# Second modulation moved behind the transposes, twelve row places, and new orders on all engines of an AdaLN block with experts

## The chip, the cores and the metric

The kernel runs on one core of one Trainium2 chip. TensorE (PE) multiplies, VectorE (DVE) and ScalarE (ACT) work elementwise, GpSimd (POOL) does small elementwise work and issues the indirect DMAs, SyncE (SP) issues most other DMAs. The metric is the device time of one execution in microseconds (us), the median of several; lower is better.

## What is computed

The input x is 2 batches x 2048 tokens x 128 channels. Cut to what matters:

```
mod = (silu(c) @ wmod).reshape(2, 6, 1, 128);  sa, ca, ga, sb, cb, gb = mod's six parts
ga, gb = sign * maximum(abs(.), 0.25)
h = layernorm(x) * (1 + ca) + sa
gate_x, gate_a = sigmoid(h @ w_in), sigmoid(h @ w_a)        # block diagonal, 8 blocks
log_a = -8 * softplus(a_param) * gate_a;  a = exp(log_a)
b = sqrt(1 - exp(2 * log_a)) * (gate_x * h)
x = x + ga * scan(a, b)                                     # y[t] = a[t] * y[t-1] + b[t]
h = layernorm(x) * (1 + cb) + sb
logits = silu(h @ rw1 + rb1) @ rw2 + rb2                    # 128 -> 512 -> 8 experts
top two experts per token, weights = softmax of the two logits
out = sum over both of weight * (silu(h @ w1[e] + b1[e]) @ w2[e] + b2[e])   # 128 -> 512 -> 128
x = x + gb * out
```

"Second modulation" is the step `* (1 + cb) + sb` on the second h. cb and sb differ by batch.

## The kernel before

**Tiles.** The 4096 tokens are 8 groups (g) of 512, four tiles of 128 tokens each; groups 0 to 3 are batch 0, groups 4 to 7 batch 1. Everything up to the experts (the head) goes by groups: LN1 statistics (`stats1`), 1/sigma (`rstd1`, POOL), normalising (`norm1`: groups 0 to 2 on POOL, the rest on DVE), transposes (`turn_x`, PE), first modulation out of PSUM (`modulate`, ACT), two gate products (`gates`, PE), `tanh` and `decay` (ACT), 1 - exp (`clamp`, an ACT Relu) and its root (`mult`, ACT), gated input and `scan` (DVE), transposes back (`turn_y`), residual and LN2 statistics (`resid`, DVE). LN2's normalising is `norm2` (DVE): two passes over each 128-token tile, L816 with 1 + cb spread over all tokens (`cbB`) and L823 with 1/sigma and sb (`sbB`). The result lies by tokens in `rows`, already modulated. It is turned (`turn_h`), copied out of PSUM by ACT (`copy`, L626), and goes through the router (`router`, `silu`, `logits`, `lgc`, `sum`). `top2` (DVE) picks two experts, `rank` (PE) counts, and `place` (DVE) works out for every token and choice a row in `sorted_rows` in HBM. POOL sends the rows there: `send`, 64 indirect DMAs at L550, each of 128 rows; those of a group wait for its `place`.

**Experts.** The sorted rows make 39 tiles of 256 rows, each for one expert. Tiles 0 to 8 hold rows of groups 0 to 3 alone (all batch 0), and can run before the second half is routed. For tile s: SP loads the rows into one of U = 10 places of `xr` (L411; a place is free when the scatter of the tile that used it has landed), PE turns them (`tx`, L1194) into bank 1, DVE copies them to `xT` (L986), and copies the expert's weights (`w1` L995, `w2` L1004; both need a register load from the table `tab`, L979), PE does layer 1 (`l1`, L1205), ACT Silu (`hid`, L657), PE layer 2 (`l2`, L1218), ACT the bias (`yb`, L666), PE turns back (`ty`, L1226) into the same bank 1, DVE scales (`sc`, L1012), POOL scatters to `expert_out` by two indirect DMAs (L559). `tx` waits until bank 1 was read by the `sc` ahead of it, `ty` until it was read by the `xT` ahead of it.

**Order.** Each engine's order is written out by hand in a table PLAN (names as above, the number is the group or tile). It ends with tile 10; then each engine runs fixed steps: 20 steps in a hardware loop, the others written out. A step s is, on PE, `tx` s+1, `l1` s, `ty` s-2, `l2` s-1; on DVE `xT` s+1, `w1` s+1, `sc` s-2, `w2` s; on ACT `yb` s-2, `hid` s. In six late steps DVE also sums up finished groups (`combine`, L1031 to L1033). A waiting instruction blocks all that stands behind it on its engine.

The reader will need these lines:

```
FIRST = 11            # first step outside PLAN
pe.wait_ge(TILE_READ[...], ...)      # ty waits s_xT, tx waits s_yo: both use bank 1
if not (static(s) and s < U):
    sp.wait_ge(s_sc[u], 16 * HALVES * (rounds(s, u) - 1))     # a load waits for its place
```

## Time and profile before

| | |
|---|---|
| median of 3 runs | 290.06 us (289.06 to 291.38) |
| profiled execution | 288.09 us, span in the trace 286.2 us |
| PE busy | 248.1 us (87%), 1179 matmul records |
| DVE busy | 188.4 us (66%), 750 instructions |
| ACT busy | 166.5 us (58%), 322 instructions |
| POOL busy | 171.6 us (60%), 192 instructions |

The profile also gives the busy share of each engine in 40 equal slices of the span (9 is 90% or more) and the granted TensorE clock in tenths:

```profile
PE   7767759997599798999999999999999999989910
DVE  3959999999999987576444444444444446866533
ACT  4189979999785355545555555555555556445300
POOL 4996211267777757777777777644554445645650
PEclk9997979999779799999999999999999999999995
```

One slice is 7.2 us. The head takes the first 15 slices or so, and the expert tiles most of the rest.

### The profile page before, as it was taken

To read this page: it belongs to the slowest core of one execution; us is meant where nothing else is said; L and a number is where in the kernel's file an instruction comes from. 1 tells how busy PE (TensorE), PEld (TensorE's weight loads), DVE (VectorE), ACT (ScalarE), POOL (GpSimd) and SP (SyncE) were. 2 spreads that over 40 slices of the span, in tenths; PEclk is the share of its full clock that TensorE was granted. 3 is DMA by queue.
4 is the path that set the end of the run, shared out by engine and by line. 5 is a ranking of instruction groups with operands and counts; after the bars stand their busy time and mean duration, and the time that the engine had idled before them with its cause. 6 is when DMAs were issued, how large, how long until landed. Compare 5 with 4: busy or idle time off the path is not lost.

```text
span 286.2 us, 4950 instructions
## 1 busy us (share of the span) xinstructions
PE 248.1 (87%) x1179; PEld 178.0 (62%) x1179; DVE 188.4 (66%) x750; ACT 166.5 (58%) x322; POOL 171.6 (60%) x192
## 2 busy tenths in 40 slices
PE   7767759997599798999999999999999999989910
PEld 6424334444144245687878888888888888868700
DVE  3959999999999987576444444444444446866533
ACT  4189979999785355545555555555555556445300
POOL 4996211267777757777777777644554445645650
PEclk9997979999779799999999999999999999999995
DMA  7993011121131226413533333222217822280505
GB/s 222 308 333 117 19 40 38 37 75 50 55 121 48 89 82 157 114 47 115 149 84 85 111 101 109 57 75 75 74 46 214 221 72 74 84 256 4 161 0 147
DMA packets 45365, 30.51 MB, mean 107 GB/s; under 512 B 5085, under 2 KB 41999, under 8 KB 45342
## 3 DMA queue, kind: packets, MB, share of 16 engines
q1 hardware_dynamic: 40432, 21.75, 27.9%
q0 software_dynamic: 4544, 8.47, 9.0%
q8 instruction: 8, 0.13, 0.2%
q14 instruction: 15, 0.12, 0.2%
q10 hardware_dynamic: 366, 0.04, 0.1%
HBM read 16.39 MB, written 12.67 MB: 102 GB/s over the span
## 4 chain that ended last, share of the span: by engine, by line
PE 40%; POOL 27%; issue 14%; DVE 12%; DMA 4%; POOLq 1%; DVEq 0%; SPq 0%; ACT 0%
POOL sorted_rows L550 21%; PE bank L1218 18%; PE bank L1205 18%; POOL shared L514 3%; PE bank L1226 3%; PE bank L1194 2%; DVE st L698 2%; DMA expert_out<-shared,tx 2%; POOL rs L506 1%; DVE shared L718 1%; POOL expert_out L559 1%; DVE tx L792 1%; DMA xs<-in_L_attn_x_dram 1%; DVE xs L803 1%; DMA tx<-sorted_rows 1%
## 5 line engine op out<-in xcount | busy, mean ns | idle before, releaser
L559 POOL DMA_INDIRECT expert_out<-shared,tx x78 | 80.4, 1031 | 52.9 <-DVE shared L1012 37.4
L657 ACT ACTIVATE hT<-bank,w_t 128x256 f32<-128x256 f32 x156 | 65.4, 470 | 29.3 <-PE bank L1205 28.3
L550 POOL DMA_INDIRECT sorted_rows<-rows,sloti x64 | 63.9, 999 | 27.2 <-issue 18.3
L1205 PE MATMUL bank<-xT,w_t 128*128 128x256 f32 x312 | 74.1, 380 | 0.1
L1218 PE MATMUL bank<-hT,w_t 128*128 128x256 f32 x312 | 74.1, 380 | 0.0
L1205 PEld LDWEIGHTS bank<-xT,w_t 128*128 128x128 f32 x312 | 56.3, 190 | 6.8 <-DVE w_t L995 0.7
L1218 PEld LDWEIGHTS bank<-hT,w_t 128*128 128x128 f32 x312 | 56.2, 190 | 6.2
L666 ACT ACTIVATE yT<-bank,w_t 128x256 f32<-128x256 f32 x39 | 18.4, 473 | 47.6 <-PE bank L1218 47.6
L1134 PE MATMUL bank<-h2T,rw_s 128*128 128x512 f32 x64 | 36.8, 677 | 1.7 <-ACT qv L644 1.4
L986 DVE COPY xT<-bank 128x256 f32<-128x256 f32 x39 | 16.5, 422 | 23.6 <-PE bank L1194 23.6
L1012 DVE TENSOR_TENSOR shared<-bank,tx 128x256 f32<-128x256 f32 x39 | 16.5, 423 | 21.3 <-PE bank L1226 21.2
L995 DVE COPY w_t<-w_s 128x516 f32 x39 | 17.2, 442 | 16.7 <-issue 15.9
L1004 DVE COPY w_t<-w_s 128x513 f32 x39 | 17.3, 443 | 15.3 <-issue 14.4
L1134 PEld LDWEIGHTS bank<-h2T,rw_s 128*128 128x128 f32 x64 | 10.8, 205 | 14.4 <-issue 5.9
L698 DVE BATCH_NORM_STATS2 st<-xs 128x6 f32<-128x128 f32 x64 | 15.7, 282 | 4.2 <-DMA xs<-in_L_attn_x_dram 4.1
L1226 PE MATMUL bank<-ident,yT 128*128 128x128 f32 x78 | 15.2, 276 | 2.5 <-ACT yT L666 1.1
L1194 PE MATMUL bank<-ident,tx 128*128 128x128 f32 x78 | 15.2, 276 | 1.8 <-DMA tx<-sorted_rows 1.3
L1226 PEld LDWEIGHTS bank<-ident,yT 128*128 128x128 f32 x78 | 10.3, 141 | 8.3 <-issue 3.3
L1194 PEld LDWEIGHTS bank<-ident,tx 128*128 128x128 f32 x78 | 10.4, 141 | 7.7 <-DMA tx<-sorted_rows 2.3
L644 ACT ACTIVATE qv<-bank,smallbT 128x512 f32<-128x512 f32 x16 | 10.8, 686 | 6.3 <-PE bank L1134 6.2
L506 POOL TENSOR_TENSOR rs<-ve,half_neg 128x4 f32<-128x4 f32 x8 | 9.3, 1164 | 8.0 <-DVE ve L705 8.0
L542 POOL TENSOR_TENSOR rs<-ve,half_neg 128x4 f32<-128x4 f32 x4 | 4.1, 1035 | 15.7 <-DVE ve L705 15.7
(194 smaller groups left out, 328.9 us busy)
## 6 DMA issues: line engine op xcount, KB each, us to landing
tx<-sorted_rows SPq DMA_DIRECT2D x39, 130.0 KB, 2.2
w_s<-in_L_ffn_w_dram SPq DMA_DIRECT2D x16, 256.0 KB, 6.1
xs<-in_L_attn_x_dram SPq DMA_DIRECT2D x8, 256.0 KB, 5.2
rows<-rows SPq DMA_DIRECT2D x8, 256.0 KB, 2.6
av<-expert_out SPq DMA_DIRECT2D x8, 256.0 KB, 3.7
qv<-expert_out SPq DMA_DIRECT2D x6, 256.0 KB, 5.0
expert_out<-shared,tx POOLq DMA_INDIRECT x78, 2.3
sorted_rows<-padr SPq DMA_DIRECT2D x9, 130.0 KB, 3.0
```

The lines of the kernel that those rows point to most:

```text
L550: p.indirect_dma_start(sorted_rows[:, :], bass.IndirectOffsetOnAxis(ap=sloti[:, k, t:t + 1], axis=0), rows[:, t, k, :], None).then_inc(s_d ...
L559: p.indirect_dma_start(expert_out[:, :], bass.IndirectOffsetOnAxis(ap=xr_i[:, s % U, n, D + 1:D + 2], axis=0), yo[:, s % U, n, :], None, b ...
L657: ins = nc.scalar.activation(hsT[:, u % 2, h, :], bank[4 + q][:, (h % 2) * SL:(h % 2 + 1) * SL], ACT.Silu, bias=w1_t[:, u % 2, HID + h:HID ...
L666: nc.scalar.activation(yT[:, u % 2, :], bank[7][:, 0:SL], ACT.Identity, bias=w2_t[:, u % 2, HC * D:W2E]).then_inc(s_yT_e, 1)
L698: ins = v.bn_stats(st[:, t, :], xs[:, t, :])
L995: v.tensor_copy(w1_t[:, u % 2, :], w1_s[:, bass.ds(e * WE, WE)]).then_inc(s_w1t, 1)
L1004: v.tensor_copy(w2_t[:, u % 2, :], w2_s[:, bass.ds(e * W2E, W2E)]).then_inc(s_w2t, 1)
L1134: t.matmul(bank[2 + n % 2][:, :], rw1_s[:, h * P:(h + 1) * P], h2T[:, g % 2, :], start=True, stop=True).then_inc(s_rl1, 1)
L1194: ins = t.transpose(bank[1][:, n * P:(n + 1) * P], xr[:, u, n, 0:D], ident[:, :])
L1205: ins = t.matmul(bank[4 + h // 2][:, (h % 2) * SL:(h % 2 + 1) * SL], w1_t[:, u % 2, h * P:(h + 1) * P], xT[:, u % 2, :], start=True, stop= ...
L1218: ins = t.matmul(bank[7][:, 0:SL], w2_t[:, u % 2, h * D:(h + 1) * D], hsT[:, u % 2, h, :], start=(h == 0), stop=(h == HC - 1))
L1226: ins = t.transpose(bank[1][:, n * P:(n + 1) * P], yT[:, u % 2, n * P:(n + 1) * P], ident[:, :])
```

## The change

1. **Second modulation on turned tiles.** `norm2` is now one pass (subtract mean, times 1/sigma), so `rows` holds unmodulated values; `sbB` and `cbB` are gone. In the turned layout cb and sb are one value per partition (`gac[:, 3]`, `modc[:, 3]`, from two small products `mod2`). The router's `copy` becomes an ACTIVATE with scale and bias, and `xT` a TENSOR_SCALAR instead of a COPY.
2. **Split column.** A tile from 9 on may hold rows of both batches. `xT` then takes two instructions: all 256 columns with batch 0's values, and again from column k on with batch 1's, k read into a register from a third row of `tab`. `table1` to `table3` have a few instructions more for it.
3. `w2` copies move from DVE to ACT.
4. **Twelve places** for loaded rows (SLOTS), so tiles 10 and 11 wait for no scatter; from tile 12 on the distance is ten as before. PLAN reaches one tile further.
5. `norm1` on POOL is now that of groups 4, 5 and 6. `clamp` of groups 0 to 3 is a POOL minimum with 1.0 (L534 of the changed kernel), with the rest folded into `mult`.
6. The unread products that open the program (`warm`) are 1 + 1 + 1 with 512 columns instead of 4 + 4 + 3 with 128.
7. PLAN is another order on every engine.

The core of the diff:

```diff
-    FIRST = 11
+    FIRST = 12
+    SLOTS = 12
-                turn_x:0 gates:0 turnb:0 turn_x:1 gates:1 turn_x:2 turn_x:3 gates:2 turn_x:4 turn_y:0
+                turn_x:0 turn_x:1 gates:0 gates:1 turn_x:2 mod2:0 turnb:0 turn_x:3 gates:2 gates:3
...
+            def slot(s):
+                return U + s if s < SLOTS - U else s % U
...
+            def no_more_than_one(g):
+                pool.wait_ge(s_exp, g + 1)
+                p.tensor_scalar(qv[:, cols(g)], qv[:, cols(g)], 1.0, None, ALU.min).then_inc(s_up, 1)
...
             def router_copy(g):
...
-                nc.scalar.copy(h2T[:, g % 2, :], turn_bank("turn_h", g)[:, :]).then_inc(s_h2T, 1)
+                nc.scalar.activation(h2T[:, g % 2, :], turn_bank("turn_h", g)[:, :], ACT.Identity,
+                                     bias=modc[:, 3, b:b + 1], scale=gac[:, 3, b:b + 1]).then_inc(s_h2T, 1)
...
+            def weights2(s, u):                                  # on ScalarE
+                e = act.value_load(tab[0:1, 1, bass.ds(s, 1)], min_val=0, max_val=NE - 1)
+                nc.scalar.copy(w2_t[:, u % 2, :], w2_s[:, bass.ds(e * W2E, W2E)]).then_inc(s_w2t, 1)
...
             def ln2_norm(g):
-                    ins = v.scalar_tensor_tensor(rows[:, t, 0, 0:D], xs[:, t, :], mv2[:, t, 0:1], cbB[:, b, :],
-                                                 ALU.subtract, ALU.mult)
-                yield from link(ins)
-                    ins = v.scalar_tensor_tensor(rows[:, t, 0, 0:D], rows[:, t, 0, 0:D], rs2[:, t:t + 1],
-                                                 sbB[:, b, :], ALU.mult, ALU.add)
+                    ins = v.tensor_scalar(rows[:, t, 0, 0:D], xs[:, t, :], mv2[:, t, 0:1], rs2[:, t:t + 1],
+                                          ALU.subtract, ALU.mult)
...
             def take_x(s, u):
-                v.tensor_copy(xT[:, u % 2, :], bank[1][:, 0:SL]).then_inc(s_xT, 1)
+                early = static(s) and s < EARLY
+                v.tensor_scalar(xT[:, u % 2, 0:SL], bank[1][:, 0:SL], gac[:, 3, 0:1], modc[:, 3, 0:1],
+                                ALU.mult, ALU.add).then_inc(s_xT if early else s_xa, 1)
+                if not early:
+                    k = dve.value_load(tab[0:1, 2, bass.ds(s, 1)], min_val=0, max_val=SL)
+                    dve.wait_ge(s_xa, s - EARLY + 1)
+                    v.tensor_scalar(xT[:, u % 2, bass.ds(k, SL)], bank[1][:, bass.ds(k, SL)], gac[:, 3, 1:2],
+                                    modc[:, 3, 1:2], ALU.mult, ALU.add).then_inc(s_xT, 1)
...
             def keep_warm(n):
-                for _ in range((4, 4, 3)[n]):
-                    t.matmul(bank[4][:, 0:P], ident[:, :], ident[:, :], start=True, stop=True)
+                for _ in range((1, 1, 1)[n]):
+                    t.matmul(bank[4][:, :].rearrange("p (k q) -> p k q", q=P), ident[:, :],
+                             ident[:, :].unsqueeze(1).to_broadcast([P, 512 // P, P]), start=True, stop=True)
```

Where instructions move, first on DVE, in one step of the hardware loop. Before (L986 `xT`, L995 `w1`, L1012 `sc`, L1004 `w2`; TENSOR_LOAD and ISA rows are register work of the queue):

```order
L985 REGISTER_ALU [waits s_txp]
L986 COPY xT<-bank 128x256 [waits s_l1]
L979 ISA
L979 TENSOR_LOAD tab
L979 ISA x2
L995 ISA [waits s_hs]
L995 COPY w_t<-w_s 128x516
L1012 TENSOR_TENSOR shared<-bank,tx 128x256 [waits s_yturn]
L979 TENSOR_LOAD tab
L979 ISA x2
L1004 ISA [waits s_yT_e]
L1004 COPY w_t<-w_s 128x513
```

The same step of the changed kernel (L1036 and L1041 are the two halves of `xT`):

```order
L1032 REGISTER_ALU [waits s_txp]
L1036 TENSOR_SCALAR xT<-bank,gac,modc 128x256 [waits s_l1]
L1039 ISA
L1039 TENSOR_LOAD tab
L1039 ISA x2
L1040 REGISTER_ALU
L1041 ISA [waits s_xa]
L1041 TENSOR_SCALAR xT<-bank,gac,modc 128x256
L1026 ISA
L1026 TENSOR_LOAD tab
L1051 ISA [waits s_hs]
L1051 COPY w_t<-w_s 128x516
```

The register load that stood behind `xT` now has a second one ahead of it, and `xT` is whole only behind the first. `w2` is gone.

Next on ACT, from the first router Silu (L644, of group 0) to the first `share` (L649, tdl). Before:

```order
L644 ACT_TABLE_LOAD [waits s_rl1]
L644 ACTIVATE av<-bank,smallbT 128x512 [waits s_y]
L644 ACTIVATE av<-bank,smallbT 128x512 [waits s_rl1]
L626 COPY h2T<-bank 128x512 [waits s_h2t]
L615 ACTIVATE qv<-qv,gac 128x512 [waits s_exp]
L644 ACTIVATE qv<-bank,smallbT 128x512 [waits s_rl1]
L634 ACTIVATE lgT<-bank,rb_c 128x512 [waits s_rw,s_lgT]
L600 ACTIVATE tx<-bank 128x512 [waits s_exp,s_z]
L601 ACTIVATE shared<-bank 128x512
L615 ACTIVATE qv<-qv,gac 128x512 [waits s_exp]
L592 ACTIVATE hT<-bank,modc,gac 128x512 [waits s_xnT]
L649 ACTIVATE tdl<-dlt 128x4 [waits s_dlt]
```

The changed kernel at the same place (L671 Silu, L633 `clamp`, L652 `copy`, L643 `mult`, L661 `lgc`, L676 `share`):

```order
L671 ACTIVATE av<-bank,smallbT 128x512 [waits s_y]
L633 ACTIVATE qv<-qv,gac 128x512 [waits s_exp]
L652 ACTIVATE h2T<-bank,modc,gac 128x512 [waits s_h2t]
L671 ACTIVATE av<-bank,smallbT 128x512 [waits s_rl1]
L643 ACT_TABLE_LOAD
L643 ACTIVATE qv<-qv 128x512 [waits s_u]
L661 ACTIVATE lgT<-bank,rb_c 128x512 [waits s_rw,s_lgT]
L643 ACTIVATE qv<-qv 128x512 [waits s_u]
L671 ACT_TABLE_LOAD
L671 ACTIVATE qv<-bank,smallbT 128x512 [waits s_rl1] x2
L676 ACTIVATE tdl<-dlt 128x4 [waits s_dlt]
```

`mult` of groups 4 and 5 came ahead of `share`, with two table loads; a `tanh`, a `modulate` and a Silu went behind it.

## Rows read from the trace of the kernel before

**Rows 1.** Stretch, length, busy of PE, PEld, DVE, ACT, POOL (instructions), clock, DMA
```profile
109.00:150.00 41.00, 39.65 (x211) 31.15 (x210) 24.11 (x103) 20.87 (x49) 31.27 (x32) 1.00 0.40 108
151.00:239.00 88.00, 88.00 (x454) 76.47 (x453) 38.25 (x91) 48.60 (x114) 52.35 (x53) 1.00 0.37 103
```

**Rows 2.** Chain that ended last, in order of time (start us, us, what)
```profile
142.63 0.96 POOL sorted_rows L550
143.89 1.00 POOL expert_out L559
145.19 2.93 DMA expert_out<-shared,tx
148.28 2.31 DMA tx<-sorted_rows
```

**Rows 3.** Timeline of POOL: first sends of two batches (start us, us, instruction, [idle before <-releaser])
```profile
58.18 1.38 POOL L550 DMA_INDIRECT sorted_rows<-rows,sloti  x1 [5.73 <-DVE sloti L864]
...
102.96 0.96 POOL L550 DMA_INDIRECT sorted_rows<-rows,sloti  x1 [2.14 <-DVE sloti L864]
```

**Rows 4.** Timeline of the SP queue, loads of expert tiles
```profile
106.08 10.05 SPq L411 DMA_DIRECT2D tx<-sorted_rows  x9
...
145.72 13.91 SPq L411 DMA_DIRECT2D tx<-sorted_rows  x6
```

**Rows 5.** Timeline of PE: tx 9, tx 10 and l1 9
```profile
149.40 0.38 PE L1194 MATMUL bank<-ident,tx 128*128 128x128 f32 x2
150.63 0.44 PE L1194 MATMUL bank<-ident,tx 128*128 128x128 f32 x2 [0.85 <-DMA tx<-sorted_rows]
150.91 1.89 PE L1205 MATMUL bank<-xT,w_t 128*128 128x256 f32 x8
```

**Rows 6.** Busy time in the head: DVE twice, then ACT
```profile
20.00:58.00 38.00, 37.02 (x165) 0.91 0.20 60
58.00:105.00 47.00, 44.76 (x234) 0.89 0.24 76
...
20.00:58.00 38.00, 35.52 (x54) 0.91 0.20 60
```

**Rows 7.** Groups of instructions by shape, page's columns
```profile
L823 DVE SCALAR_TENSOR_TENSOR rows<-rows,rs,sbB 128x128 f32<-128x128 f32 x32 | 9.4, 343 | 0.2
...
L615 ACT ACTIVATE qv<-qv,gac 128x512 f32<-128x512 f32 x8 | 5.7, 714 | 0.0
...
L626 ACT COPY h2T<-bank 128x512 f32<-128x512 f32 x8 | 4.7, 583 | 3.6 <-PE bank L1057 3.6
...
L620 ACT ACT_TABLE_LOAD x4 | 5.1, 1283 | 0.1
...
L493 POOL TENSOR_SCALAR_AFFINE_SELECT wx_bd<-wx_c 128x128 f32<-128x128 f32 x1 | 0.3, 346 | 0.0
```

**Rows 8.** One line: POOL's normalising, duration ns min/median/max, first and last start
```profile
L514 POOL TENSOR_SCALAR shared<-xs,mv,rs x12: 784/793/1135, 6.2 to 18.6; 128x128 f32<-128x128 f32 x12
```

**Rows 9.** Timeline of ACT: the first router Silu
```profile
47.88 1.27 ACT L644 ACTIVATE av<-bank,smallbT 128x512 f32<-128x512 f32 x2
```

**Rows 10.** Timeline of one loop step, PE and DVE
```profile
201.54 1.89 PE L1205 MATMUL bank<-xT,w_t 128*128 128x256 f32 x8
...
201.85 0.42 DVE L986 COPY xT<-bank 128x256 f32<-128x256 f32 x1 [0.76 <-PE bank L1194]
...
202.73 0.43 DVE L995 COPY w_t<-w_s 128x516 f32 x1 [0.46 <-issue]
...
203.27 0.38 PE L1226 MATMUL bank<-ident,yT 128*128 128x128 f32 x2
```

**Rows 11.** Timeline of a step with a sum: xT late, then ty
```profile
241.90 0.42 DVE L986 COPY xT<-bank 128x256 f32<-128x256 f32 x1
...
242.46 0.41 PE L1226 MATMUL bank<-ident,yT 128*128 128x128 f32 x2
```

**Rows 12.** Register work of DVE's queue, min/median/max ns
```profile
L979 DVEq TENSOR_LOAD <-tab x44: 301/314/516, 155.0 to 238.8; - x44
```

More of the change, by code:

```diff
@@ L230, in adaln_block @@
         s_out = sem("s_out")
-        s_sc = sems(*(f"s_sc{i}" for i in range(U)))
+        s_sc = sems(*(f"s_sc{i}" for i in range(SLOTS)))
         s_y01 = sems(*(f"s_y01_{g}" for g in range(NG)))
@@ L618, in multiplier @@
             def multiplier(g):
-                act.wait_ge(s_u, g + 1)
-                nc.scalar.activation(qv[:, cols(g)], qv[:, cols(g)], ACT.Sqrt).then_inc(s_m, 1)
+                if g < CLAMPED:
+                    act.wait_ge(s_up, g + 1)
+                    nc.scalar.activation(qv[:, cols(g)], qv[:, cols(g)], ACT.Sqrt, bias=gac[:, 2, 0:1],
+                                         scale=-0.25).then_inc(s_m, 1)
+                else:
+                    act.wait_ge(s_u, g - CLAMPED + 1)
+                    nc.scalar.activation(qv[:, cols(g)], qv[:, cols(g)], ACT.Sqrt).then_inc(s_m, 1)
             def router_copy(g):
@@ L921, in early_table @@
                 dve.wait_ge(s_cnt, 1)
+                v.tensor_copy(first[:, :], bank[7][:, 0:NE])
                 yield from link(v.tensor_tensor(cmpk[:, :, :, :], bank[7][:, 0:NE].unsqueeze(2).unsqueeze(3)
@@ L1083, in modulation, with modulation2 @@
                 ins.then_inc(s_modc, 1)
+            def modulation2(_):
+                pe.wait_ge(s_modok, 1)
+                for i in range(3, 5):
+                    ins = t.matmul(bank[6][:, i * B:(i + 1) * B], wmod_s[:, i * D:(i + 1) * D], csil[:, :],
+                                   start=True, stop=True)
+                ins.then_inc(s_modc, 1)
             def modulation_rows(_):
-                pe.wait_ge(s_modok, 1)
+                pe.wait_ge(s_modok, 2)
                 pe.wait_ge(s_csb, 1)
@@ L1185, in turn_table @@
                 pe.wait_ge(s_tile, 1)
-                for k in range(2):
+                for k in range(3):
                     ins = t.transpose(table_bank()[:, k * LATE:(k + 1) * LATE], tile_p[:, k:k + 1], ident[0:LATE, 0:LATE])
```

238 lines of the change are left out of this document (130 added, 108 removed).

## The prediction

> **What bounds the kernel now.** I read the page's slices first, then the busy time by stretches, the chain of waits, and the timelines around the places that these named. Three stages have three different limits.
>
> From 151 to 239 us PE is busy for 88.00 of 88.00 us, DVE for 38 and ACT for 49 [rows 1]. In this stretch only what makes PE wait, or gives it less to do, counts. The change takes no PE work out of a tile.
>
> Ahead of it the chain runs along POOL: 64 sends one behind another, the last starting at 142.63, then the scatter of tile 0, its landing (2.93 us), and the load of tile 10 (2.31 us), which had waited for tile 0's place [rows 2]. PE got to `tx` 9 at 149.40, sat idle 0.85 us, turned tile 10 at 150.63 and began `l1` 9 at 150.91 [rows 5]. From there to the end PE's work is fixed. So the head is worth what it moves `l1` 9. But from 109 to 150 us PE was busy 39.65 of 41 us [rows 1]: POOL's chain ends last by little, and a gain needs POOL and PE both earlier.
>
> What starts POOL's chain? The first send ran at 58.18 and had waited 5.73 us for DVE's `place` of group 0; the send at 102.96 waited 2.14 us for `place` of group 4 [rows 3]. Between these a send takes what POOL takes. From 20 to 58 us DVE is busy for 37.02 of 38 us and ACT for 35.52, and from 58 to 105 DVE for 44.76 of 47 [rows 6]. So the head hangs on DVE and ACT, and through them POOL and PE.
>
> **The change, part by part.** The sum is made on the profiled execution (288.09 us with a span of 286.2); the median of the runs is 290.06, 1.97 above, and I carry the difference over to it.
>
> *First send.* Ahead of `place` of group 0 DVE loses the second pass of `norm2` (L823, 0.343 us an instruction [rows 7]). The old order had three groups with both passes there, 24 instructions, the new one has four groups with one, 16. With four fewer reads of PSUM for the spread rows that is 12 x 0.343 = 4.1 us at most. ACT is the later of the two. Ahead of its first `share` it loses four clamps (to POOL), two of `tanh`, a `modulate` and a Silu: eight instructions, gains two `mult`, net six x 0.714 = -4.3 us; it gains two table loads, 2 x 1.283 = +2.6, and two copies with scale and bias at no more than 0.714 - 0.583 each, +0.3 [rows 7]. Net -1.4 us. Of ACT's 2.5 us of idle time [rows 6] I let 2.0 go, since DVE now normalises groups 0 to 3 where POOL needed 4 x 0.793 = 3.2 us a group [rows 8]. Together -3.4: first send at 54.8. Bounds: 0 (POOL late, the second rival) and -5.5 (DVE's 4.1 and part of the early waits).
>
> *Sends of batch 1.* DVE has four groups times four L823 less, 16 x 0.343 = 5.5 us, before `place` of group 4, but `table1` has been put ahead of it. I take 1.2 of the 2.14 us of waiting as gone (bounds 0 and 1.84; 0.3 is the usual gap).
>
> *Tile 10.* With twelve places its load waits for no scatter. The last send ended at 143.59 and the next load was issued at 145.72, 2.13 us later; loads follow at 10.05/9 = 1.1 us [rows 2, 4]. New: sends end at 143.59 - 3.4 - 1.2 = 139.0, loads of tiles 9 and 10 at 141.1 and 142.2, landing 2.2 later at 144.4, `l1` 9 at 144.7. That is -6.2 us against 150.91. Without the places, scatter 0 would hold it to about 146. Tile 12 needs scatter 2: it starts 4.6 us earlier, as do all behind the sends, and PE wants it 6.2 us earlier; POOL's two scatters a tile take 2 x 1.3 = 2.6 us [rows 2] against PE's 3.9 (454 records in 88 us, 20 a tile [rows 1]), which covers this.
>
> *PE before that.* It must be at `tx` 9 by about 143.4. Loads 0 to 8 began at 106.08 [rows 4], late because `table1` and group 7's `norm2` stood at the end of DVE's queue. With 3.4 us from the start and 5.5 less the earlier table they begin some 5 to 6 us earlier, and PE has one router product and one logit sum fewer among them. 149.40 - 5.5 - 1.5 = 142.4: enough by 1 us.
>
> *The split `xT`.* This is the loss. `ty` s-2 waits until bank 1 was read by all of `xT`. In a loop step `l1` starts at 201.54, `xT` at 201.85 (+0.31), the copy behind its register load at 202.73 (0.88 later), and `ty` at 203.27 (+1.73) [rows 10]. The second half of `xT` sits behind the same kind of load with one register instruction more, as the order shows. I take 0.93 to its start, and 0.45 for itself: 0.42 is `xT` now, 0.48 with two operands per partition. Where `xT` was late before, it ended at 242.32 and `ty` started at 242.46, 0.14 later [rows 11]. So `ty` could start at 0.31 + 0.93 + 0.45 + 0.14 = 1.83: 0.10 late, and some 0.03 for weights that were not loaded ahead. In the 20 loop steps, 20 x 0.13 = +2.6 us. The written-out steps have no index to compute, and I count nothing. Bounds: 0 if the load overlaps a little more, and 0.3 a step (6 us) if it is as slow as its longest, 516 ns against 314 [rows 12].
>
> The Trainium skill (DMA: Bandwidth & Descriptors, Latency and other measured facts) gives a `tensor_load` a floor of about 600 ns. This case's row has a median of 314 ns; by the page each step would be late by 0.29 more, the loop by 5.7 us more, and the time would be 292. The row decides.
>
> *Steps with sums.* DVE bounds them: three sums' instructions, then `xT` late [rows 11]. `w2` leaves them (a copy and its load) and half an `xT` with a second wait comes: I count 0, and 1 us either way. *`w2` on ACT:* ACT has 48.60 busy of 88 us [rows 1], and 22 copies at no more than 0.714 make it 64: hidden. If ACT were late for `yb`, `ty` would be next; it has over 1 us. *Warm products:* the 11 x 128 columns become 3 x 512, about the same columns, ahead of the first transposes: 0. *Tail:* unchanged.
>
> Sum: -6.2 + 2.6 = -3.6 us; span 282.6, profiled execution 284.5, median **286.5 us**.
>
> **The rivals.**
>
> *Second half hidden.* If the load gets going while the first half runs, so that 0.82 instead of 0.93 passes, `ty` is on time. All of -6.2 stays: 283.9 us. For it: the written-out steps show shorter loads.
>
> *POOL becomes late.* It now does four minima on 512 columns and the normalising of groups 4 to 6 while DVE and ACT wait for it. A minimum's price is unknown: 4 x 0.346 = 1.4 us if it is like the select of 128 columns, 4 x 0.793 = 3.2 if like the normalising [rows 7, 8]. I take it below 2, as it has no operands per partition. At 3.2, 4 x 1.8 = 7.2 us more stand ahead of group 6's normalising, whose `modulate` stands ahead of the first Silu on ACT (47.88 now [rows 9], 10.3 ahead of the first send); POOL's slack takes some 2, the rest delays the first send, and with it goes most of the head's gain: -6.2 + 5 + 2.6, 291.5 at worst, about 290 in the middle. One of 12 normalising instructions took 1135 ns against a least of 784 while both engines worked [rows 8].
>
> The Trainium skill (SBUF — State Buffer, SBUF: two separate sides) says that DVE and GpSimd lock a shared pair of ports against each other when DVE has two SBUF inputs and GpSimd reads SBUF. That is the case for the scans and gated inputs against the minima; it would act as this rival does, and the 1135 ns agrees with it.
>
> *PE is the limit of the head.* If PE doesn't come earlier than its 149.40 by more than 2 us (a late `lgc` behind the two new table loads, say), `l1` 9 begins at 147.5 or so: -3.4 + 2.6, 289.3.
>
> *The split costs more than the head gives: slower.* The place is `ty` in each loop step. It decides from a loss of 9.1 us in 20 steps, 0.45 a step, which brings -6.2 to +2.9. That needs the second half to begin 1.25 us behind the first instead of 0.93. Against it: the register loads above. For it: the half waits on a semaphore of DVE itself, and then for two computed addresses. At 0.6 a step it is 295.9; I price the case at 293.
>
> **How the numbers follow.** Forecast 0.45 (285 to 288.5); hidden half 0.15; POOL late 0.18; PE the limit 0.12; slower 0.10. A measurement of this kernel can tell about 1% from no change, that is 287.2 and 293.0. Faster by over 1%: most of the forecast (0.36) and the hidden half: 0.51. Slower by over 1%: half of the last rival and the worst of POOL's with a loop loss on top, 0.10. Same: 0.39. The range leaves out the slower half of the last rival and the luckiest tenth: 282.8 to 291.3.
>
> **What would show it.** First send near 54.8 (between 53 and 58); little waiting at group 4's; `l1` 9 at 144 to 146 with PE idle for a microsecond or two ahead of it; in the loop `ty` 1.83 us behind `l1` and a period near 4.03 us instead of 3.90. Wrong would be: minima of 3 us on POOL with ACT waiting for them, PE busy without a gap up to `l1` 9, or a period over 4.3.

## The result and the profile after

The change made the kernel slower. The table gives the median of all executions and the ratio to the kernel before on the same chips.

| | before | after |
|---|---|---|
| median | 290.21 us (288.67 to 291.44) | 295.31 us (293.91 to 296.68) |
| ratio | 1 | 1.0175 (95%: 1.0124 to 1.0226) |
| profiled execution, span | 288.09 us, 286.2 us | 293.91 us, 292.1 us |

I had forecast 286.5 us with a range up to 291.3, and the likeliest sign was wrong. Three places in the two traces show where the 5.9 us of span are. First before: layer 2 of tile 8 (the first behind the gap), layer 2 of tile 30 (20 loop steps behind tile 10), and the last bias on ACT. The columns of every timeline here are start us, us, instruction, [idle before <-releaser].

```profile
152.85 1.46 PE L1218 MATMUL bank<-hT,w_t 128*128 128x256 f32 x6
...
238.54 1.25 PE L1218 MATMUL bank<-hT,w_t 128*128 128x256 f32 x5
...
272.57 0.47 ACT L666 ACTIVATE yT<-bank,w_t 128x256 f32<-128x256 f32 x1 [2.26 <-PE bank L1218]
```

The same places after, and layer 2 of tile 10, the last that no loop step has touched:

```profile
153.73 1.46 PE L1270 MATMUL bank<-hT,w_t 128*128 128x256 f32 x6
...
161.52 0.81 PE L1270 MATMUL bank<-hT,w_t 128*128 128x256 f32 x3
...
245.12 1.89 PE L1270 MATMUL bank<-hT,w_t 128*128 128x256 f32 x8
...
278.49 0.47 ACT L706 ACTIVATE yT<-bank,w_t 128x256 f32<-128x256 f32 x1 [2.26 <-PE bank L1270]
```

| stretch | predicted | measured |
|---|---|---|
| start to `l2` 8 | -6.2 | +0.88 |
| 20 loop steps | +2.6 | 83.60 - 20 x 3.895 = +5.70 |
| the rest | 0 | 5.92 - 6.58 = -0.66 |

**The loop.** One step on the chain of waits (start us, us, what; DVEq is the register work of DVE's queue):

```profile
197.24 0.08 DVE xT L1036
...
197.36 0.47 DVEq L1039
...
197.85 0.19 DVEq L1039
...
198.29 0.56 DVE xT L1041
198.84 0.04 issue
198.89 0.44 PE bank L1278 x2
```

The load of k (L1039) starts 0.12 us behind the first half and takes 0.47 us in this step; register arithmetic of 0.19 us and the address computation follow, so the second half starts 1.05 us behind the first. It ends at 198.85, and `ty` comes right behind it. The two halves on DVE:

```profile
197.24 0.54 DVE L1036 TENSOR_SCALAR xT<-bank,gac,modc 128x256 f32<-128x256 f32 x1 [1.50 <-PE bank L1246]
198.29 0.54 DVE L1041 TENSOR_SCALAR xT<-bank,gac,modc  x1 [0.50 <-DVE xT L1036]
```

The 20 steps of the loop are not alike. The load took 301 to 314 ns in six of them and 411 to 473 in fourteen, always issued 0.12 us behind the same instruction (two stretches of the loop; duration ns min/median/max, first and last start):

```profile
L1039 DVEq TENSOR_LOAD <-tab x3: 304/310/314, 168.5 to 176.6; - x3
L1039 DVEq TENSOR_LOAD <-tab x10: 411/455/473, 180.7 to 218.6; - x10
```

With a short load the halves start 0.93 to 0.97 us apart and a step takes 4.05 to 4.10 us; with a long one, 1.00 to 1.11 us and 4.12 to 4.23. The first steps of the two rounds (the hardware loop has two rounds of ten steps) are apart by 1.35 and 1.28 us and take 4.57 and 4.50.

PE's busy share doesn't tell this: from 151 to 239 us it is still 86.73 of 88 us, but with 421 matmul records where [rows 1] had 454. The third row of this view (stretch, length, busy of PE, PEld, DVE, ACT, POOL, clock, DMA) has it, the first is the head:

```profile
20.00:58.00 38.00, 29.02 (x102) 14.51 (x101) 32.90 (x152) 33.11 (x47) 24.90 (x23) 0.87 0.23 70
109.00:150.00 41.00, 36.57 (x201) 30.30 (x201) 22.72 (x98) 24.30 (x56) 31.40 (x32) 1.00 0.39 109
151.00:239.00 88.00, 86.73 (x421) 70.23 (x421) 38.22 (x83) 55.73 (x126) 48.35 (x50) 0.99 0.35 97
```

**The head.** DVE was busy 37.02 of 38 us before [rows 6] and is busy 32.90 now; ACT fell from 35.52 to 33.11. Both have less to do, and both wait. The timelines of POOL, PE and DVE show for what:

```profile
22.72 4.09 POOL L528 TENSOR_SCALAR shared<-xs,mv,rs 128x128 f32<-128x128 f32 x4
26.77 1.18 POOL L520 TENSOR_TENSOR rs<-ve,half_neg 128x4 f32<-128x4 f32 x1
28.06 3.59 POOL L528 TENSOR_SCALAR shared<-xs,mv,rs 128x128 f32<-128x128 f32 x4
...
31.70 1.11 PE L1102 MATMUL bank<-ident,shared 128*128 128x128 f32 x4 [3.76 <-POOL shared L528]
32.61 1.92 PE L1162 MATMUL bank<-hT,wx_bd 128*128 128x512 f32 x2
34.32 1.91 PE L1163 MATMUL bank<-hT,wa_bd 128*128 128x512 f32 x2
36.02 1.06 PE L1102 MATMUL bank<-ident,hT 128*128 128x128 f32 x4
...
37.12 0.69 DVE L850 TENSOR_TENSOR xs<-bank,xs 128x512 f32<-128x512 f32 x1 [2.19 <-PE bank L1102]
```

PE stands 3.76 us for group 5's normalising on POOL, with `gates` 4 queued behind it, though its input was ready at 28.33 (`modulate` 4 on ACT). The two products of `gates` 4 (L1162, L1163) then take 1.9 us each, where 1.02 is the time at the full clock: from 32.6 to 36.0 us the granted clock is 0.50. So `turn_y` 1, whose input was ready at 32.37 (`scan` 1), starts only at 36.02, and DVE waits 2.19 us for it. The kernel before has such a place too: 1.92 and 1.33 us for the products at 40.19 and 41.90, behind 4.84 us of idle time. The first send comes at 59.31 instead of 58.18 [rows 3]; the last starts at 142.43 instead of 142.63 [rows 2].

**The gap ahead of the fixed steps.** PE's timeline, the counterpart of [rows 5]:

```profile
143.19 1.89 PE L1270 MATMUL bank<-hT,w_t 128*128 128x256 f32 x8
147.92 0.44 PE L1246 MATMUL bank<-ident,tx 128*128 128x128 f32 x2 [2.83 <-DMA tx<-sorted_rows]
149.86 0.65 PE L1246 MATMUL bank<-ident,tx 128*128 128x128 f32 x2 [1.51 <-DVE xT L1041]
150.30 3.37 PE L1257 MATMUL bank<-xT,w_t 128*128 128x256 f32 x8
153.51 0.38 PE L1278 MATMUL bank<-ident,yT 128*128 128x128 f32 x2
```

PE had done `l2` 7 by 145.08 (143.19 + 1.89), 4.3 us earlier than before (`tx` 9 at 149.40 followed it without idle time [rows 5]). It then waits 2.83 us for tile 9's load and 1.51 for `xT` 9's two halves, and `l1` 9, though it starts 0.6 us earlier than before, takes 3.37 us instead of 1.89.

### The profile page after: what moved, and what is told of

Read it like the earlier page. It is cut to its first block, busy times and chain, and to the rows that moved or that the text cites. A ratio compares the mean times of both kernels' runs of the same rounds, so it can differ in the third digit from the quotient of the medians.

```text
span 292.1 us, 5113 instructions
## 1 busy us (share of the span) xinstructions
PE 252.1 (86%) x1168; PEld 174.9 (60%) x1168; DVE 184.5 (63%) x714; ACT 189.8 (65%) x361; POOL 179.6 (61%) x196
## 4 chain that ended last, share of the span: by engine, by line
PE 34%; POOL 25%; issue 15%; DVE 12%; DMA 5%; DVEq 4%; ACT 2%; SPq 1%; POOLq 1%; ACTq 0%
POOL sorted_rows L568 20%; PE bank L1270 15%; PE bank L1257 9%; PE bank L1278 4%; DVEq L1039 3%; DVE xT L1041 3%; POOL shared L528 3%; PE bank L1246 2%; DMA xs<-in_L_attn_x_dram 2%; DVE st L739 1%; DVE xT L1036 1%; PE bank L1162 1%; PE bank L1102 1%; PE bank L1163 1%; DMA tx<-sorted_rows 1%
## 5 line engine op out<-in xcount | busy, mean ns | idle before, releaser
L577 POOL DMA_INDIRECT expert_out<-shared,tx x78 | 79.3, 1016 | 60.2 <-DVE shared L1059 44.9
L568 POOL DMA_INDIRECT sorted_rows<-rows,sloti x64 | 64.9, 1014 | 26.3 <-issue 18.9
L1257 PE MATMUL bank<-xT,w_t 128*128 128x256 f32 x312 | 75.5, 386 | 0.1
L1257 PEld LDWEIGHTS bank<-xT,w_t 128*128 128x128 f32 x312 | 57.6, 194 | 6.9 <-DVE w_t L1051 0.3
L1036 DVE TENSOR_SCALAR xT<-bank,gac,modc 128x256 f32<-128x256 f32 x39 | 21.2, 543 | 43.4 <-PE bank L1246 42.4
L1186 PE MATMUL bank<-h2T,rw_s 128*128 128x512 f32 x64 | 35.1, 652 | 3.1 <-ACT qv L671 1.5
L700 ACT COPY w_t<-w_s 128x513 f32 x39 | 24.2, 619 | 1.1 <-ACT yT L706 0.9
L1041 DVE TENSOR_SCALAR xT<-bank,gac,modc x30 | 16.3, 544 | 12.0 <-DVE xT L1036 11.6
L1186 PEld LDWEIGHTS bank<-h2T,rw_s 128*128 128x128 f32 x64 | 10.4, 195 | 18.0 <-issue 10.5
L1278 PEld LDWEIGHTS bank<-ident,yT 128*128 128x128 f32 x78 | 8.7, 141 | 15.1 <-DVE xT L1041 9.1
L520 POOL TENSOR_TENSOR rs<-ve,half_neg 128x4 f32<-128x4 f32 x8 | 8.7, 1093 | 8.0 <-DVE ve L746 7.9
L1102 PE MATMUL bank<-ident,shared 128*128 128x128 f32 x32 | 6.7, 345 | 7.9 <-POOL shared L528 4.8
```

Source lines behind the costliest of these rows:

```text
L568: p.indirect_dma_start(sorted_rows[:, :], bass.IndirectOffsetOnAxis(ap=sloti[:, k, t:t + 1], axis=0), rows[:, t, k, :], None).then_inc(s_d ...
L577: p.indirect_dma_start(expert_out[:, :], bass.IndirectOffsetOnAxis(ap=xr_i[:, slot(s), n, D + 1:D + 2], axis=0), yo[:, slot(s), n, :], Non ...
L700: nc.scalar.copy(w2_t[:, u % 2, :], w2_s[:, bass.ds(e * W2E, W2E)]).then_inc(s_w2t, 1)
L1036: v.tensor_scalar(xT[:, u % 2, 0:SL], bank[1][:, 0:SL], gac[:, 3, 0:1], modc[:, 3, 0:1], ALU.mult, ALU.add).then_inc(s_xT if early else s_ ...
L1041: v.tensor_scalar(xT[:, u % 2, bass.ds(k, SL)], bank[1][:, bass.ds(k, SL)], gac[:, 3, 1:2], modc[:, 3, 1:2], ALU.mult, ALU.add).then_inc(s ...
L1186: t.matmul(bank[2 + n % 2][:, :], rw1_s[:, h * P:(h + 1) * P], h2T[:, g % 2, :], start=True, stop=True).then_inc(s_rl1, 1)
```

## The experiments

Theories at the start: A, the split `xT` costs the loop's 5.7 us, and most of it is the register load; B, POOL's new work holds the head; C, idle time ahead of `l1` 9 is paid twice, by the idle time and by a lower clock; D, the twelve places bring little. Each kernel is the changed kernel with the edit shown. Each ratio is to the kernel before on the same chip.

### Theory A: the load moved, the second half left out

```diff
             def take_x(s, u):
+                early = static(s) and s < EARLY
+                if not early:
+                    k = dve.value_load(tab[0:1, 2, bass.ds(s, 1)], min_val=0, max_val=SL)
                 dve.wait_ge(s_txp, s + 1)
...
                 if not early:
-                    k = dve.value_load(tab[0:1, 2, bass.ds(s, 1)], min_val=0, max_val=SL)
                     dve.wait_ge(s_xa, s - EARLY + 1)
```

> The changed kernel, with the register load that the second half of `xT` needs moved ahead of `take_x`'s first wait, where DVE idles 1.50 us a step. Nothing else changes. In the changed kernel the halves of a loop step start 1.02 to 1.05 us apart and take 0.54 each, `ty` starts 1.92 us behind `l1`, and a step takes 4.15 us against 3.90 before. Theory A (the loop's loss of some 5 us is DVE's second half arriving late, and the load between the halves is the part of it that can be hidden): the halves start 0.6 to 0.7 us apart, `ty` 1.73 us behind `l1`, the period falls to 3.90 to 3.95, the time to 290.3 to 291.3 (1.000 to 1.004 of before). Rival A2 (what separates the halves is the wait on DVE's own semaphore and the computed addresses, the load runs under the first half): the gap stays near 1.0, the period at 4.10 or more, the time at 294.5 to 295.5. Rival A3 (the loop is slower for another reason, such as `w2` on ACT): the gap shrinks but the period stays at 4.1.

Measured: 289.49 us, ratio 0.9968 (0.9921 to 1.0015). The halves in the loop:

```profile
199.46 0.54 DVE L1038 TENSOR_SCALAR xT<-bank,gac,modc 128x256 f32<-128x256 f32 x1 [1.60 <-PE bank L1247]
200.19 0.55 DVE L1042 TENSOR_SCALAR xT<-bank,gac,modc  x1 [0.18 <-DVE xT L1038]
```

They start 0.73 us apart, `ty` is 1.73 us behind `l1`, and a step takes 3.895 us again. One move of one load gave back 5.7 us in the loop and 2% of the time (0.9968 against 1.0175). A holds and A2 falls: the wait and the addresses alone leave DVE idle for 0.18 us. The time is 0.8 us below the expected range; in this trace `l1` 9 took 1.89 us, not 3.37, which the moved load does not explain (see theory C). In the steps with sums, where DVE has no idle time, the load moved ahead is not hidden: 4.34 to 4.59 us a step there against 4.23.

> The changed kernel with the second half of `xT` (and its register load and wait) left out of all tiles from 9 on, so the rows of batch 1 are not modulated as they should be: it measures the whole price of the split. Theory A: the period of a loop step is back at 3.90, the steps with sums are each some 0.3 us shorter, tile 10 is turned 1 us earlier, and the time is 289 to 290 (0.995 to 1.0). Rival A3 (`w2` on ACT or the twelve places make the loop slower): the period stays over 4.0 and the time over 293.

Measured: 284.82 us, ratio 0.9802 (0.9711 to 0.9893), less than any theory had. The loop is at 3.895 us, so `w2` on ACT and the places cost it nothing, and A3 falls. The steps with sums are at 3.895 too, where I had expected 0.3 us less each (it is 0.33): five of them give 1.7 us. The profiled executions are 7.9 us apart (293.91 and 286.02), of which the loop and these steps are 7.4. The medians are 10.5 apart, from two groups of runs and with four executions here; the rest is not placed. So the split costs more than the whole loss: without it the kernel would have been 2% faster than before.

### Theory C: products that nobody reads, in the gaps

```diff
-                ... l2:7 tx:9 tx:10
+                ... l2:7 warm:3 tx:9 tx:10            # three products of 512 columns into bank 2
```

> The changed kernel with three products of 512 columns on TensorE that nobody reads, ahead of `tx` 9, where PE is idle for 2.83 us for the load of tile 9; nothing else. Theory C (the idle time costs a second time, because the clock is granted at half after it): `l1` 9 takes 1.9 us instead of 3.37, and `ty` 7 and `l2` 8 come 1.0 to 1.4 us earlier, and with them all the rest; the time is 293.9 to 294.3. Rival C2 (what follows `l1` 9 waits for something else, such as ACT's Silu or the places): `l1` 9 takes 1.9 us and `l2` 8 still starts at 153.7; time 295.3. Rival C3 (the clock falls for another reason): `l1` 9 stays near 3.4.

Measured: 293.69 us, ratio 1.0088 (1.0044 to 1.0132). In the profiled execution, itself 3 us above that median, the load landed late: 1.89 us of idle time stayed ahead of `tx` 9 and 1.51 behind it, and `l1` 9 took 3.62 us. Inconclusive; so both gaps were filled, beside the changed kernel once more.

> The changed kernel as it is, once more, as the reference of the three others of this group, since the first send has come anywhere from 57.8 to 59.6 in kernels with the same head. All theories expect 293.5 to 296.5, 1.010 to 1.022 of before, and the trace as it was within the spread of the head.

Measured: 295.13 us, ratio 1.0121 (1.006 to 1.0182). First send at 60.21, `l1` 9 2.90 us.

> The changed kernel with unread products of 512 columns on TensorE in both gaps of tile 9 and 10: three ahead of `tx` 9 and one between `tx` 9 and `tx` 10. Three alone left 1.89 us of idle time ahead of `tx` 9 (the load landed late in that run) and 1.51 behind it, and `l1` 9 stayed at 3.2 us and more, so the theory was not tested. Theory C (idle time ahead of `l1` 9 halves its clock): with less than 1.5 us of idle time in all, `l1` 9 takes 1.9 us and `ty` 7 comes 1.1 to 1.5 us earlier against the sends' end than in the changed kernel; the time is 1.0 to 1.5 us below the changed kernel's of this group. Rival C2 (something else holds what follows): `l1` 9 at 1.9 us and the same time. Rival C3: `l1` 9 over 3 us although PE was busy.

Measured: 292.73 us, ratio 1.0112 (1.0066 to 1.0158); the ratio can't be told from the changed kernel's. The trace can:

```profile
147.26 0.44 PE L1248 MATMUL bank<-ident,tx 128*128 128x128 f32 x2
147.53 1.02 PE L1122 MATMUL bank<-ident 128*128 128x512 f32 x2
149.21 0.41 PE L1248 MATMUL bank<-ident,tx 128*128 128x128 f32 x2 [0.65 <-DVE xT L1041]
149.45 1.89 PE L1259 MATMUL bank<-xT,w_t 128*128 128x256 f32 x8
151.21 0.41 PE L1280 MATMUL bank<-ident,yT 128*128 128x128 f32 x2
```

`l1` 9 takes 1.89 us, and `ty` 7 comes 8.39 us behind the end of the sends (142.82) instead of 10.12 (153.51 - 143.39). C holds in its place: 1.5 us of clock (1.00 over `l1` 9 here) and 0.2 more. In the time it is not shown. In all six later kernels of this study that had products in both gaps, e12 aside, `l1` 9 took 1.89 us as well. Idle time alone doesn't decide it, though: e1 had 2.28 us of it without filling and ran at 1.89, e2 had 2.32 and took 2.92.

### Theory D: ten places

```diff
-    SLOTS = 12
+    SLOTS = 10
```

> The changed kernel with ten places instead of twelve, so the loads of tiles 10 and 11 wait for the scatters of tiles 0 and 1 again. Theory D (the places bring nothing, since tile 9 is held by the end of the sends and tile 10 by `xT` 9's two halves): scatter 0 lands some 4 us behind the last send, tile 10's load lands 2 to 2.5 us behind that, at 148.3 to 148.8, `tx` 10 moves by less than 0.5 us from 149.9, time within 0.5 us of the changed kernel's. Rival D2 (the places carry the head's gain, as I predicted): `tx` 10 comes 1.5 us later or more, and so does everything behind it: the time is 1.5 to 3 us above the changed kernel's of this group.

Measured: 295.11 us, ratio 1.0108 (1.0047 to 1.0169).

```profile
148.62 0.44 PE L1246 MATMUL bank<-ident,tx 128*128 128x128 f32 x2 [3.10 <-DMA tx<-sorted_rows]
151.13 0.69 PE L1246 MATMUL bank<-ident,tx 128*128 128x128 f32 x2 [2.07 <-DMA tx<-sorted_rows]
```

`tx` 10 waits 2.07 us for its load where it waited 1.51 for `xT` 9. The places bring 0.56 us, about the half microsecond that theory D allowed; `tx` 10 itself starts 1.27 us later than in the changed kernel, 0.70 of it with `tx` 9. In the time they bring nothing that can be seen: 295.11 us against 295.13 for the changed kernel on the same chip (e5), four executions each. D holds.

### Theory B: which of POOL's work holds the head

```diff
-    POOLED = (4, 5, 6)
+    POOLED = (6,)                       # norm1:4 and norm1:5 in DVE's plan, behind stats1:5 and input:2
```

> The changed kernel with the normalising of groups 4 and 5 on DVE again (1.1 us a group there, 3.6 to 4.1 on POOL); group 6's stays on POOL. In the changed kernel PE sits idle 3.76 us at 31.70 for group 5's and 1.09 at 26.86 for group 4's, turns `turn_y` 1 only at 36.02 behind it, at half clock, and DVE is idle 2.19 us for that and 0.86 for POOL's rstd. Theory B (POOL's normalising holds the head): the first send comes at 55.5 to 57 instead of 59.3, all sends with it (they follow in 82.8 us whatever starts them), the last ends at 138.5 to 140, and the time falls by 1.5 to 3 us, to 292.5 to 294. Rival B2 (DVE's own work sets the first send, whose 2.2 us more eat the gap): first send 58.5 to 60, time unchanged at 295. Rival B3 (the first send comes earlier, but the gap ahead of tile 9 is then limited by the loads' start or PE): first send near 56, time within 0.5 us of 295.3.

Measured: 293.85 us, ratio 1.0101 (1.0052 to 1.0149), first send at 58.10. The waits for groups 4 and 5 are gone, but ACT now waits 2.94 us for group 6's. Only 1.2 us of the expected 2.3 to 3.8 came, and 58.10 lies within the spread of one and the same head (below). The sends ended 1.5 us earlier (141.87), but `tx` 11 came only 0.15 us earlier (155.31 against 155.46): behind 4.4 us of idle time `l1` 9 took 3.62 us at a granted clock of 0.50. The next one moved that too, with the load of e1 in all steps but those with sums, and I put two things in the wrong order.

> The changed kernel with two edits that act in different stages. (1) The register load of the second half is ahead of `take_x`'s wait in all steps but those with sums, where DVE has no idle time to hide it and the load moved ahead had made the step 4.35 to 4.6 us instead of 4.2. (2) DVE normalises groups 4, 5 and 6 as well, so POOL normalises none and takes rstd of group 1 ahead of the last minimum; with groups 4 and 5 alone the wait had gone over to group 6's (ACT idle 2.94 us) and rstd 1 (DVE idle 1.63), and the first send came only 1.2 us earlier. Theory B (POOL holds the head): both waits go, the first send comes at 55.5 to 57. Rival B2 (DVE's own work, 3.4 us more of it): first send at 58 or later. With theory A's loop (3.90 a step, sums 4.2) the time is 287 to 289 if B holds, 289 to 290 if B2 does.

Measured: 292.30 us, ratio 1.0087 (1.0048 to 1.0125), first send at 62.86: 3.5 us later than in the changed kernel.

```profile
40.63 0.72 ACT L639 ACTIVATE qv<-qv,gac 128x512 f32<-128x512 f32 x1 [5.36 <-POOL qv L534]
...
45.62 0.69 PE L1106 MATMUL bank<-ident,shared 128*128 128x128 f32 x2 [6.05 <-DVE shared L759]
```

One minimum behind one rstd on POOL cost ACT 5.36 us. For B it says nothing; the loop is at 3.895 us and the steps with sums at 4.23, as intended. The mended order, with both gaps filled:

> As e8, with the order of the head mended and the unread products of e6 in both gaps. In e8 POOL's minimum of group 3 stood behind rstd 1 (ACT idle 5.36 us for it) and DVE's normalising of group 6 stood behind `norm2` 1 (PE idle 6.05 us for it), so the first send came at 62.86 and theory B was not tested. Here both minima stand ahead of rstd 1 and `norm1` 6 stands right behind `norm2` 0. Theory B (POOL's normalising holds the head): no engine waits over 1.5 us between 26 and 45 us, first send at 55.5 to 57. Rival B2 (DVE's own work sets it): first send at 57.5 to 59 and DVE without idle time. Time by B 285 to 287, by B2 286.5 to 288.5.

Measured: 287.48 us, ratio 0.9926 (0.9886 to 0.9967), first send at 57.65. No wait on DVE between 20 and 56 us: it is B2's picture, though with POOL normalising nothing the first send came 1.7 us earlier than in the changed kernel. PE waits 1.98 us for `rowsA` on DVE, and `place` 0 then 1.34 us for PE.

> The changed kernel with its head as it is, the register load of the second half ahead of the wait in all steps without sums, and the unread products in both gaps of tiles 9 and 10. Theories A and C together: 5.4 us in the loop and 1.5 to 2 at `l1` 9 below the changed kernel, and the steps with sums at 4.2 us: 287 to 289, 0.990 to 0.998 of before. If the two don't add (the time saved ahead of the loop is lost to a wait in it), 289 to 290.5.

Measured: 287.87 us, ratio 0.9928 (0.9886 to 0.997), first send at 59.32. The time is in the expected range, with the loop at 3.895 us and `l1` 9 at 1.89, and the head is as it was. The ratio's interval overlaps e1's, so the time alone doesn't show C's share.

The minima back on ACT, on top of e10:

```diff
-    CLAMPED = 4
+    CLAMPED = 0                         # clamp:0 to clamp:3 in ACT's plan, none in POOL's
```

> As e10, with the four minima of batch 0 back as clamps on ACT (four instructions of 0.71 us), so POOL keeps only the normalising of groups 4 to 6. It tells which of POOL's new work holds the head. If it is the minima (1.49 to 1.79 us each), the normalising of group 5 ends some 3 us earlier, PE's idle 3.7 us at 31 go, and the first send comes at 56 to 57.5: the time is 1 to 2 us below e10's. If it is the normalising (3.6 to 4.1 us a group, and it starts when DVE's statistics of group 4 are there, at 21.5, not when the minima are done), the waits ahead of `turn_x` 4 and 5 stay, ACT has 2.8 us more to do, and the first send comes at 59.5 to 61: the time is 1 to 2.5 us above e10's.

Measured: 286.68 us, ratio 0.9898 (0.9861 to 0.9936), first send at 56.51. This is the first branch, with two thirds of its size: group 5's normalising ends at 29.63 instead of 31.65, and PE still waits 2.78 us for it. Behind this wait the products of `gates` 4 took 1.02 us each. The ratio's interval overlaps e10's; the trace carries the reading.

> As e11 (minima on ACT, the load ahead of the wait, unread products in both gaps; 0.9898 of before), with the normalising of group 4 on DVE, 1.1 us there against 3.8 on POOL. In e11 PE still sat idle 2.78 us at 29.68 for group 5's normalising on POOL, which ran behind group 4's, and ACT 0.61 and 0.72. If POOL's two in a row are what is left, group 5's ends some 3 us earlier, the first send comes at 55.3 to 56.2 instead of 56.51 and the time is 0.5 to 1 us below e11's, 0.985 to 0.989 of before. If DVE's 1.1 us more outweigh it (with all three groups on DVE the first send came at 57.65 with no idle time on DVE), first send at 56.5 to 57.6 and the time at e11's or up to 1 us above.

Measured: 332.73 us, but the kernel before took 332.19 us on that chip as well, and its trace has three stretches of 1.6 to 2.0 us in which no engine works. Nothing follows from it. It was run again with two others.

> The kernel of e12 again, on another chip: minima on ACT, the load ahead of the wait, unread products in both gaps, and group 4 normalised on DVE (1.1 us there, 3.8 on POOL). In e11 PE sat idle 2.78 us at 29.68 for group 5's normalising, which runs behind group 4's on POOL. If that wait holds the head, it falls below 0.5 us and the first send comes 0.5 to 1.2 us earlier than in e15; if DVE's own work holds it, the wait goes as well and the first send comes at e15's or up to 1.1 us later.

> As e13, with groups 5 and 6 normalised on DVE too, so POOL has none of the new work, only the rstds; `rowsA` stands ahead of `norm2` 2, since PE had waited 1.98 us for it in e9. If POOL's normalising still holds the head, the first send comes 1 us or more earlier than in e15; if DVE is the bound once the minima are gone, 3.4 us more on DVE bring it 1 to 3 us later than in e15 with DVE idle for less than 1 us between 20 and 56, and the time 1 to 3 us above e15's.

> The kernel of e11 again, as the reference of this group. If its gain over e10 was the minima and not the spread of the head, the first send comes at 56 to 57.5 again and the time is 0.986 to 0.993 of before; if it was the spread, first send at 58 to 59.5 and 0.991 to 0.997.

| kernel | us | ratio (95%) | first send |
|---|---|---|---|
| e13, group 4 on DVE | 285.78 | 0.9858 (0.9813 to 0.9904) | 57.94 |
| e14, all on DVE | 285.05 | 0.9817 (0.9756 to 0.9879) | 57.30 |
| e15, minima on ACT alone | 287.00 | 0.9887 (0.9852 to 0.9923) | 57.32 |

The first send doesn't come earlier with less on POOL than e15 left it; both branches that expected it fall. e14's other branch, a later send and a longer time, falls as well. In e14 the engine that is full is plain (20 to 56 us, columns as above):

```profile
20.00:56.00 36.00, 27.98 (x98) 13.17 (x98) 33.88 (x158) 35.80 (x52) 10.26 (x8) 0.91 0.23 68
```

ACT is busy for 35.80 of 36 us and DVE for 33.88. The eight traces with the head of the change have the first send at 57.82 to 60.21, 59.19 in the mean; the four with the minima on ACT at 56.51 to 57.94, 57.27 in the mean. So the minima on POOL cost some 2 us, though the spread of one and the same head is over 2 us itself. They are not the only way to that: e9 kept them, took the normalising off, and had 57.65. Taking either off POOL brought the first send to 57 or 58; in e14 ACT is the limit, with DVE close behind; in e15 neither is full (33.80 and 31.55 of 36 us), and what holds its first send near 57 is not shown. Why e13 and e14 have lower medians than e15 is not settled. Their intervals overlap, and one place behind the sends differs in the traces: PE waits 1.96 us for tile 9's load in e15 and not at all in e13 and e14.

e14 is the fastest version found that leaves nothing out: it beats the kernel before by 1.8% and the changed kernel by some 10 us. It has four executions, and its interval overlaps those of e13 and e15.

## Why the prediction was wrong

**The head's first send, -3.4 (measured +1.1).** The step that failed is "Of ACT's 2.5 us of idle time [rows 6] I let 2.0 go, since DVE now normalises groups 0 to 3", with the slack that the POOL rival gave POOL. DVE's and ACT's work did shrink, but the change put POOL between them: its minima and its normalising wait for one another in one queue, and the idle time between 20 and 58 us rose from 2.5 to 4.9 us on ACT and from 1.0 to 5.1 on DVE. The minimum itself was priced right:

```profile
L534 POOL TENSOR_SCALAR qv<-qv x4: 1486/1490/1873, 17.7 to 35.1; 128x512 f32<-128x512 f32 x4
```

(duration ns min/median/max.) 1.49 us lies between my ends of 1.4 and 3.2 and below 2. What failed is the slack that I gave POOL, "some 2 us": from 17.7 to 43.7 us its timeline has four minima (6.3 us together), twelve normalisings (11.3) and six powers of 1.0 to 1.6, and 0.8 us of idle time. That is the rival "POOL becomes late", which I gave 0.18. The rival had the wrong reason, though (a minimum of 3.2 us), so its sign was right partly by luck. It was also not the whole miss: with POOL freed, the first send came at 57.3, not at 54.8. I had added up savings of DVE and ACT apart, as though the slower of the two set the time, where each waits for the other by way of PE.

Part of POOL's lateness is that DVE and POOL hold each other up. A POOL instruction that starts while DVE runs an instruction with two inputs in SBUF takes longer:

```profile
24.15 1.27 DVE L844 TENSOR_TENSOR_SCAN hT<-av,tx 128x512 f32<-128x512 f32 x1
24.68 1.34 POOL L528 TENSOR_SCALAR shared<-xs,mv,rs 128x128 f32<-128x128 f32 x1
```

That is 1.34 us instead of 0.80. In the changed kernel five of POOL's sixteen new instructions are longer (the normalisings of 1175, 1257, 1317 and 1341 ns and the minimum of 1873), 2.3 us together, 1.8 of them ahead of group 5's end; each starts during a scan of DVE or one of the products ahead of it (L831, L839), and none of the other eleven does. All kept traces but e12's agree: of 188 normalisings and minima on POOL 61 were longer by over 60 ns, and exactly these 61 start so. The other way, DVE's normalising takes longer while a minimum is in progress on POOL (first the four behind 33.2 us, where one runs, then twelve where none does):

```profile
L862 DVE TENSOR_SCALAR rows<-xs,mv,rs x4: 334/581/710, 33.2 to 34.3; 128x128 f32<-128x128 f32 x4
L862 DVE TENSOR_SCALAR rows<-xs,mv,rs x12: 322/341/349, 44.8 to 55.4; 128x128 f32<-128x128 f32 x12
```

Six instructions of DVE lose 1.7 us in this way (three at 18.1 to 19.2 us, three of the four shown), and with the minima on ACT (e11) none does. That is about what the first send gained by moving them.

The Trainium skill (SBUF — State Buffer, SBUF: two separate sides) has DVE and GpSimd lock each other out of a shared pair of ports, and I had put that beside this rival. The traces agree. The medians hide it: POOL's normalising has a median of 804 ns here and 793 before [rows 8]. How much of the head's loss is this and how much the full queue, no run separates.

**The sends of batch 1, -1.2 (measured -1.33).** The size is right: from first to last send 83.12 us instead of 84.45. The parts are not: all of the 2.14 us of waiting [rows 3] is gone, not 1.2, but the 64 sends themselves took 1.0 us longer (64.9 us together instead of 63.9).

**Tile 10 and the places.** The step "loads of tiles 9 and 10 at 141.1 and 142.2 ... `l1` 9 at 144.7" has `tx` 10 wait for its load alone. It waits for `xT` 9, now two instructions with a load between them: 1.51 us, and 1.45 even with the load moved (e1). The places, which I had credited with 1.3 us (146 against 144.7), are worth 0.56 (e7).

**`l1` 9's length.** I had written "PE idle for a microsecond or two ahead of it" as a sign of success and gave it no price. It had one, 1.48 us. The granted clock of four stretches (the clock is the number behind POOL's): the idle one, the two turns, `l1` 9, and what follows:

```profile
145.00:148.00 3.00, 0.17 (x2) 0.09 (x2) 0.00 (x0) 1.09 (x2) 2.39 (x3) 1.00 0.42 98
148.00:150.30 2.30, 0.79 (x4) 0.58 (x5) 1.09 (x2) 0.00 (x0) 1.69 (x3) 0.91 0.60 160
150.40:153.40 3.00, 3.00 (x9) 2.37 (x9) 1.09 (x2) 0.84 (x2) 2.39 (x3) 0.52 0.21 66
154.00:157.00 3.00, 3.00 (x17) 2.61 (x16) 1.23 (x3) 1.79 (x5) 2.37 (x3) 1.00 0.45 125
```

**PE before that.** Predicted ready at 142.4, measured 145.08; the loads 0 to 8 began at 104.67, 1.4 us earlier instead of 5 to 6. It didn't decide, since tile 9 landed later still.

**The split `xT`, +2.6 (measured +5.7).** The mechanism was right, the size was off. `ty` was due at 1.73 us behind `l1`, and I had 1.83. In the five steps with a short load (the loop's first one left out) it came at 1.83 to 1.87: the 0.93 to the second half's start was right there. What was short is the half itself, 0.54 us and not 0.45, made good by the 0.04 and not 0.14 from its end to `ty`; the 0.48 that I gave an instruction with two operands per partition stands in no row. Even so these steps lost 0.15 to 0.21 us and not 0.13, since layer 2 starts 0.27 us behind a late `ty` instead of 0.22. In the thirteen steps with a long load `ty` came at 1.90 to 2.01, and they lost 0.22 to 0.34. The first steps of the two rounds lost 0.67 and 0.60. That makes 0.9 + 3.5 + 1.3 = 5.7 us, 0.285 a step; the bound of 0.3 a step held in the mean.

The load's size is a term that [rows 12] did not show rightly. They mix two places: in the kernel before, the loop's 20 loads right behind `xT` took 303 to 516 ns, with a median of 334, and the 20 behind `sc` 301 to 316. I had taken the median of both, with the maximum as the bound. Why the same load takes 0.31 us in one step and 0.46 in another stays open; it is not that DVE is busy, since the next load (L1026), issued 0.11 us behind the second half while it runs, has a median of 309 ns.

The Trainium skill (DMA: Bandwidth & Descriptors, Latency and other measured facts) gives a `tensor_load` about 600 ns. Here the loads between the halves took 301 to 473 ns. The time that I had worked out from the page, 292, was nearer to the result than mine, but not for its reason.

**Steps with sums, 0 (measured -0.66 for the whole rest).** Right: 4.23 us a step against 4.17 to 5.0 before. **`w2` on ACT, tail, warm products:** nothing seen of them, as predicted; `w2` takes 0.619 us on ACT, and e2's loop of 3.895 us shows it hidden.

**The rivals.** "The split costs more than the head gives" had the right sign. It was to decide from 0.45 us a step, since I set it against a head gain of 6.2 us; with a head gain of nothing, the measured 0.285 was enough. I had treated the rivals as separate cases, and two of them came true together. Each rested on a price that I had only bounded, so the range should have held their sum: 290.06 + 5.7 with no gain of the head is 295.8, 0.5 us from what was measured. That it comes so near is partly luck, since `l1` 9's 1.5 us of clock are not in it.

## What to carry to other kernels

A register load between two instructions that need each other is not hidden by the first: here it put 0.2 to 0.4 us between them. If the register is known earlier, load it ahead of the wait in which the engine idles anyway, and only there: in a step without idle time it is one instruction more on the path. Work handed to an engine "with slack" is paid for by everyone who waits for it in its queue, so add up that engine's queue in order of time between its first and last deadline, not its busy share. On POOL add what DVE's scans and products of two tensors in SBUF hold up, and on DVE what POOL's do; look at the maximum of a group and not only at its median. Where a stage is fed by a chain, being early for it earns nothing, and on TensorE it may cost the clock of what comes next.
